# Last tiles one by one, earlier second gate and up weights, and a later weight turn in a four-stage network on one core

## The reference, cut to what matters

```python
x = x + ln(attn0(ln(x)))   # stage 1: per-token attention, Wq and Wkv
x = x + ln(ffn0(ln(x)))    # stage 2: ternary weights w1, w2, w3 (1408 hidden)
x = x + ln(attn1(ln(x)))   # stage 3: causal attention, 16 heads, RoPE
x = x + ln(ffn1(ln(x)))    # stage 4: gate and up 512x2048, 2:4 sparsified, down 2048x512

def quantize(w):           # of stage 2
    gamma = mean(abs(w))
    return clip(round(w / (gamma + 1e-8)), -1, 1)

def ffn1(x):
    h = silu(x @ w_gate) * (x @ w_up)
    h = keep_two_largest_of_every_four(h)      # by magnitude
    return h @ w_down
```

## Time and profile before

| | us |
|---|---|
| median of three runs | 1434.9 |
| range of the runs | 1433.83 to 1436.38 |
| the profiled execution | 1431.71 |
| its span, first to last instruction | 1430.0 |

### The profile page before, as it was taken

The page is one execution under the profiler, slowest core; times in us unless marked ns, Lnnn a source line. Parts: engine busy times, 40 slices in busy tenths (PEclk is TensorE's granted clock), DMA queues, the critical chain, the costliest instruction groups (busy, mean ns, idle before and its releaser), DMA issues.

```text
span 1430.0 us, 19458 instructions
## 1 busy us (share of the span) xinstructions
PE 1348.8 (94%) x7206; PEld 918.9 (64%) x7206; DVE 973.9 (68%) x1959; ACT 661.3 (46%) x1151; POOL 698.8 (49%) x836
## 2 busy tenths in 40 slices
PE   6988999999989899989999999999999999999996
PEld 5875445555455454555554447788888888888885
DVE  5997475755657776676665534577668767886776
ACT  6654233231314554445463574455454645454442
POOL 2676131421313323234243366487678768766863
PEclk9999999999999899999999999999999999999998
DMA  9100110203213111134020411522223232432300
GB/s 336 63 1 1 74 59 16 89 1 96 74 44 97 53 46 49 35 86 143 3 75 10 135 58 60 205 89 89 89 89 147 99 114 98 158 122 88 118 30 29
DMA packets 46270, 116.86 MB, mean 82 GB/s; under 512 B 3420, under 2 KB 4448, under 8 KB 42336
## 3 DMA queue, kind: packets, MB, share of 16 engines
q1 hardware_dynamic: 45104, 114.31, 23.8%
q10 hardware_dynamic: 1072, 1.31, 0.3%
HBM read 92.28 MB, written 23.07 MB: 81 GB/s over the span
## 4 chain that ended last, share of the span: by engine, by line
PE 65%; DVE 22%; ACT 5%; POOL 3%; issue 3%; DMA 1%; SPq 0%; POOLq 0%; DVEq 0%; ACTq 0%
PE PS L1657 63%; DVE cm L626 4%; DVE SM L642 3%; DVE PS L829 2%; DVE SM L638 2%; PE PS L1666 1%; DVE tm L626 1%; ACT EX L1241 1%; DVE hm L635 1%; DVE SM L643 1%; DMA rw<-in_L_ffn_w_up 1%; POOL xA L1472 1%; POOL SM L1472 1%; DVE SM L632 1%; DVE hm L626 1%
## 5 line engine op out<-in xcount | busy, mean ns | idle before, releaser
L1241 ACT ACTIVATE EX<-PS 128x512 f32<-128x512 f32 (+3 forms) x384 | 170.2, 495 | 154.9 <-PE PS L1657 153.9
L1472 POOL TENSOR_TENSOR ws_g<-rw,ws_g 128x512 fp32r<-128x512 f32 x64 | 138.5, 2164 | 124.8 <-ACT ws_g L1062 124.8
L1472 POOL TENSOR_TENSOR SM<-SM 128x1 f32<-128x1 f32 x128 | 82.5, 644 | 233.3 <-DVE SM L632 230.5
L1657 PE MATMUL PS<-KG,QG 96*128 96x512 f32 (+3 forms) x384 | 141.1, 392 | 21.5 <-DVE SM L829 9.0
L1576 POOL TENSOR_SCALAR_AFFINE_SELECT EX<-EX 128x128 f32<-128x128 f32 x256 | 75.3, 303 | 161.7 <-ACT EX L1241 158.3
L829 DVE CUSTOM_DVE_ANT_0 PS<-PS,MW 128x128 f32<-128x128 f32 (+3 forms) x256 | 122.4, 500 | 43.9 <-PE PS L1657 43.3
L1657 PE MATMUL PS<-QG,KG 98*128 98x512 f32 (+3 forms) x384 | 135.6, 382 | 3.2 <-ACT EX L1241 3.0
L1441 ACT ACTIVATE ab<-hm 128x512 f32<-128x512 f32 x64 | 40.5, 633 | 203.6 <-DVE hm L626 203.6
L1657 PE MATMUL PS<-ws_d,HH 128*128 128x512 f32 x528 | 125.7, 389 | 0.7 <-DVE HH L626 0.7
L638 DVE TENSOR_REDUCE SM<-PS 128x1 f32<-128x512 f32 x128 | 87.7, 686 | 55.4 <-PE PS L1657 55.1
L1657 PEld LDWEIGHTS PS<-QG,KG 98*128 98x128 f32 x384 | 72.0, 192 | 76.2 <-issue 45.3
(11 more groups left out here) (204 smaller groups left out, 2798.7 us busy)
## 6 DMA issues: line engine op xcount, KB each, us to landing
rw<-in_L_ffn_w_gate SPq DMA_DIRECT2D x16, 1024.0 KB, 5.1
rw<-in_L_ffn_w_up SPq DMA_DIRECT2D x16, 1024.0 KB, 5.1
rw<-in_L_ffn_w_down SPq DMA_DIRECT2D x16, 1024.0 KB, 6.9
QG<-qs SPq DMA_DIRECT2D x48, 256.0 KB, 4.5
raw<-in_L_ffn_w SPq DMA_DIRECT2D x3, 2816.0 KB, 11.7
qs<-stg SPq DMA_DIRECT2D x16, 512.0 KB, 3.5
xA<-xs SPq DMA_DIRECT2D x2, 2048.0 KB, 8.8
ys<-xA SPq DMA_DIRECT2D x4, 1024.0 KB, 5.9
```

The source lines that it names most:

```text
L1241: e.activation(EX[:, n % 16, 0:W], PS[:, score_bank(n), 0:W], ACT.Exp, scale=ISQ, bias=0.0).then_inc(S["ex"], 1)
L1472: return e.tensor_tensor(out, a, b, op)
L1657: return e.matmul(out, l, r, start=start, stop=stop, skip_group_check=free)
```

## The change

Four things change, and no instruction that computes is added or removed.

- **Turns at stage 2.** Blocks 0 and 1 of piece 11 of w3 are no longer turned at step 19. PE turns block 0 between `turn_x(1)` and `turn_x(2)` and blocks 1 and 2 after `turn_x(3)`. ACT copies all three after its four `turn_x`.
- **High and low parts first.** In each step of `project`, ACT's `out_hi` stands ahead of `norm6`, and DVE's `out_lo` ahead of the statistics.
- **Second gates and ups sooner; turns.** SP asks for g1 and u1 right after u0, ahead of the two row writes and the read of `xb[1]`. Their wait is now for the last weighing (`pvd` 96) and the last use of `RD` (`oo` 16). The first two turns of stage 4 (`turn4(0)`, `turn4(1)`) wait for the last exponential and no longer for the draining of the last weighed banks.
- **End.** PE runs the last four groups tile by tile. DVE takes the statistics of tile i+1 ahead of the addition of tile i, and those of tile 0 ahead of `last_low(1)`.

```diff
@@ sp_program
             w.wait_ge(S["st"], NS)
             e.dma_start(rw4[:, 1, :].rearrange("p (c i) -> p c i", c=4), wu_v[0]).then_inc(S["d_r1"], 16)
-            for half in range(2):
-                w.wait_ge(S["ey"], 8 + 4 * half + 4)
-                e.dma_start(ys_h[:, 8 + 4 * half:8 + 4 * half + 4, :],
-                            xc[:, 4 * half:4 * half + 4, :]).then_inc(S["d_ys1"], 16)
-
-            w.wait_ge(S["ot"], 16)
-            e.dma_start(xb[1][:, :, :], ys_h[:, 4:8, :]).then_inc(S["d_xb1"], 16)
...
                 else:
-                    w.wait_ge(S["ep"], 16)
+
+                    w.wait_ge(S["pvd"], 96)
+                    w.wait_ge(S["oo"], 16)
...
             ask("g", 1)
+            ask("u", 1)
+            for half in range(2):
+                w.wait_ge(S["ey"], 8 + 4 * half + 4)
+                e.dma_start(ys_h[:, 8 + 4 * half:8 + 4 * half + 4, :],
+                            xc[:, 4 * half:4 * half + 4, :]).then_inc(S["d_ys1"], 16)
+
+            w.wait_ge(S["ot"], 16)
+            e.dma_start(xb[1][:, :, :], ys_h[:, 4:8, :]).then_inc(S["d_xb1"], 16)
...
-                if s % 4 == 1:
+                if s % 4 == 1 and s > 1:
                     ask("u", s // 4 + 1)
@@ dve_program
             def project(step):
+                if 0 < step < 8:
+                    out_lo(1, step)
                 for k, i in stages(8, 4, step):
                     if k == 2:
                         w.wait_ge(S["ep"], 8 + i + 1)
                         stats(88 + i, PS[:, i % 4, :], EPS, "mv6")
-                    if k == 0 and i > 0:
-                        out_lo(1, i)
...
-            last_low(1)
-            for i in range(4):
+
+            def last_stats(i):
                 w.wait_ge(S["dd"], dd_at(63, i) - 3)
                 stats(124 + i, PS[:, i, :], EPS, "mv8")
+
+            def last_rows(i):
                 w.wait_ge(S["sn5"], 13 + i)
                 tt(xb[1][:, i, :], xb[1][:, i, :], row4("p", 12 + i), ALU.add).then_inc(S["xo"], 1)
+
+            last_stats(0)
+            last_low(1)
+            last_stats(1)
+            last_rows(0)
+            last_stats(2)
+            last_rows(1)
+            last_stats(3)
+            last_rows(2)
+            last_rows(3)
@@ act_program
-                if step < 21:
+                if step < 19:
                     quantized(step - 8, 0)
...
             def project(step):
+                if 0 < step < 8:
+                    out_hi(1, step)
                 for k, i in stages(8, 4, step):
                     if k == 3:
                         norm6(1, i, PS[:, i % 4, :])
-                    if k == 0 and i > 0:
-                        out_hi(1, i)
...
-            turn_x(0)
-            turn_x(1)
-            quantized(11, 1)
-            turn_x(2)
-            turn_x(3)
+            for i in range(4):
+                turn_x(i)
+            for part in range(2):
+                quantized(11, part)
@@ pe_program
-                quantized(s - 8, 0)
-                quantized(s - 8, 1)
+                if s < 19:
+                    quantized(s - 8, 0)
+                    quantized(s - 8, 1)
...
             def turn4(t):
                 w.wait_ge(S["sn4"], t + 1)
-                w.wait_ge(S["oe"], 16)
-                w.wait_ge(S["de"], 16)
+
+                w.wait_ge(S["ex"], NS)
+                if t >= 2:
+                    w.wait_ge(S["oe"], 16)
+                    w.wait_ge(S["de"], 16)
...
             turn_x(0)
             turn_x(1)
-            quantized(11, 2)
+            quantized(11, 0)
             turn_x(2)
             turn_x(3)
+            quantized(11, 1)
+            quantized(11, 2)
...
-            for half in range(2):
+            for i in range(4):
                 for q in range(60, 64):
-                    down4(q, (2 * half, 2 * half + 1))
+                    down4(q, (i,))
```

## The result

| | before | after |
|---|---|---|
| median of four runs, us | 1435.64 | 1421.63 |
| range of the runs | 1433.83 to 1437.64 | 1420.51 to 1426.00 |
| the profiled execution | 1431.71 | 1421.57 |
| its span | 1430.0 | 1419.8 |

The ratio after to before is 0.9899, with a 95% interval of 0.9876 to 0.9922: 14.0 us by the medians, 10.1 us by the two profiled executions. The forecast was 1422.2 us with a sum of 12.7 us. Timed again later beside the kernel before, the changed kernel was 9.7 us faster (1423.38 against 1433.12, ratio 0.9924), so the 14.0 us lie on the high side.

The account below looks back on a forecast made before the run. PE was taken to set the time from 931 us on, with losses at the entries of stages 4 and 2 and the tail. Gains 6.6 + 4.7 + 1.4 = 12.7 us gave 1434.9 - 12.7 = 1422.2 us, range 1418.0 to 1428.0.

Parts of the forecast that it names:

- Entry: Entry of stage 4: early asks and earlier PE start bring first comparison and ninth gate forward, gain 6.6 us.
- PE, not ACT, ends last, by 0.6 us: Stage 4 entry, ahead of the first comparison: PE's fourth up ends at 901.5, ACT's fourth silu at 900.9.
- The 3.1 us that ACT's order might have cost: Rival at stage 4 entry: high parts delay normalizations by 3.1 us, entry yields 3.5; 1425.3 us, chance 0.16.
- hidden: Rival at stage 4 entry: another equally long wait stands behind the transfers, entry yields 0; 1428.8 us, chance 0.07.
- PE alone: Rival: the comparison-to-ninth-gate chain shortens too and PE alone decides, 8.5 us at the entry; 1420.3 us, chance 0.08.
- End: After PE's last matmul: tile by tile, the last addition ends 3.6 us behind it; gain 4.7 us, 4 to 5.
- The step on the cover: End: tile 0's statistics, 1.09 us, fill DVE's idle time; without that cover PE's tile 2 is up to 1.1 late.
- Stage 2: Entry of stage 2: moved turns keep the clock up through the first 16 matmuls; gain 1.4 us, ends 1.6 and -0.5.
- the rests that are left there are under 1 us each: Ahead of stage 2's first dense matmul, two blocks of turns fill the 2.27 us idle time, leaving rests under 1 us.
- the clock takes back: Rival: clock falls at stage 2, gaining nothing, and at the last projection tile, losing 1.5 us; 1425.1 us, chance 0.20.
- The sum: Whole kernel: 6.6 + 4.7 + 1.4 = 12.7 us; profiled execution 1419.0, median of runs 3.2 above, 1422.2 us.
- Slower: Rival: granted clock stays at 0.50 over a long stretch of stage 4; 40 us of it give 1442, chance 0.02.

Follow-up runs that it names:

- an experiment: Changed kernel with ACT's split of the ninth gate weight ahead of group 5's absolute value and the third up weight's split a step later: 1421.79 us, ratio 0.9926.
- the eight later profiles of the other kind: Profiles with the changed kernel's end where PE's rest was 0.67 to 0.71 us and last 48 matmuls to last addition took 16.08 to 16.12 us.
- the unchanged kernel: The changed kernel run and profiled once more with no edit: 1423.38 us, ratio 0.9924 to the kernel before.
- the fill: Changed kernel with 14 unused matmuls of 512 columns added in PE's idle times around the third tile's turn at stage 2's entry: 1420.32 us, ratio 0.9918.
- the old splits: Kernels without the moved splits of the ninth gate weight and third up weight; the changed kernel with those moved took 1421.79 us, with the fill too 1421.60.

## Why the prediction was right or wrong

**Entry, right.** Forecast 6.6, measured 6.87. The step "PE, not ACT, ends last, by 0.6 us" is in the trace: DVE waits 4.61 us for PE's fourth up, and ACT's silu is over at 901.23, 1.4 us ahead of it. The first gate is 2.78 us sooner instead of 2.4, and the distance from comparison to ninth gate stayed (77.08 - 55.19 = 21.89; now 21.87), which is why the wait ahead of that gate became 1.54 us (forecast 1.9). The 3.1 us that ACT's order might have cost did not appear. The asks came later than forecast, 859.34 - 855.71 = 3.6 us behind the last weighing, since they wait for POOL's scaling; the transfers had landed by 867.04 and the first split of these weights starts at 894.67, so this cost nothing. The transfers were not hidden: the asks alone decide over 5.90 us.

**PE alone, wrong as a hope.** That rival wanted the chain behind the comparison to get shorter. It stayed at 21.9 us. When it was shortened in an experiment, 0.86 of the 1.21 us won at the gate were lost again behind it, where PE waits for DVE's products.

**End, right in its mechanism, lucky in its figure.** 4.7 forecast, 4.69 measured, 4.3 in the eight later profiles of the other kind. The forecast let the last round take 3.6 us behind PE's last matmul, as before; it took 1417.34 - 1413.30 = 4.0. In after that was made up by PE's rest, 0.32 us where the forecast kept 0.69, and that shorter rest belongs to the execution. The step on the cover, statistics of tile 0 in DVE's idle time, held, and its loss was seen where PE's order was taken back.

**Stage 2, wrong in the profile of after.** The forecast took 1.4 us and the first 16 matmuls became 0.63 us slower. The step that failed is "the rests that are left there are under 1 us each": those are 0.65 and 0.21 us, as forecast, but it counted only the rest ahead of `up2(0)` and the two blocks put into it, and set the 2.5 us that the cleared step 19 leaves ahead of the third turn apart as a condition of a rival. That rest is there, 2.21 us, and in seven of nine profiles the clock fell behind it. The rival *the clock takes back* was half right: at stage 2 it fell, at the last projection tile, after 1.20 us, it did not (12 matmuls in 2.97). Over ten profiles the part is worth 5.15 - 4.22 = 0.9 us on the mean (both profiles of the old order took 5.15), between -0.6 and 1.6, and no median shows it: it is a matter of the execution. The start of `up2(0)` was between 120.06 and 121.54 us in the twelve profiles with the turns moved and 120.40 and 120.24 in the two without, so the 0.63 lost there is within the spread.

**The sum.** 12.7 forecast less 2.66 for stage 2 (1.4 hoped for, 0.63 and 0.63 lost), plus 0.27 at the entry, less 0.16 in the stretches nothing touches, is 10.1. That the time came out at 1421.63 all the same is luck, because the second error has the other sign: the forecast added 3.2 us between the profiled execution and the median, and the profile of after took 1421.57, at its median. The profiled execution of before was a quick one of its kind, 3.9 us under the median of that comparison.

**Slower, did not come.** The clock was at 1.00 behind the ninth gate.

## What to carry over

A gain ahead of a wait is worth nothing until that wait is gone, so edits that lie on one path are costed together and tested by taking back one at a time: here 0.97 and 4.15 alone made 6.87 together, and of the end's two reorderings one alone gave nothing, the other about half. When work is moved out of one rest into another, the rest that it leaves is part of the bill: list every idle time of the engine after the move, the earlier ones too. For parts of one or two us, compare distances between points of the program, which repeated to 0.1 us at the entry here, and not the medians, whose runs spread over 2 to 7 us.

## What the runs showed of the hardware that was not expected

**The same rest, three outcomes of the clock.** After a rest of PE of 2.20 or 2.21 us, in the same order of work, the granted clock fell to 0.50 at one of two moments or not at all, and the first 16 matmuls took 3.5, 4.0 or 5.8 us. In both profiles that had the rest filled the clock stayed up. The Trainium skill, "TensorE: Matmul & The Clock Gate", section "What's actually happening", says of a kernel's start that the number of slow matmuls of one and the same kernel changes from run to run. In the middle of this one, the unchanged kernel's two profiles (5.78 and 3.51 us) agree, though in the second the rest was 1.37 us.

**The untouched stretch varies by more than any part of the change but the entry.** From `up2(1)` to the last weighing, where none of these kernels differ, the profiles took 727.8 to 733.5 us. The four longest, 733.2 to 733.5, are the four whose granted clock from 400 to 480 us is 0.87; the others have 0.91 to 0.96. The unchanged kernel profiled again, then the fill, both from 400 to 480 us:

```profile
400.00:480.00 80.00, 73.61 (x331) 42.20 (x332) 52.01 (x147) 28.44 (x53) 17.61 (x32) 0.87 0.27 73
```

```profile
400.00:480.00 80.00, 72.42 (x345) 39.81 (x350) 54.54 (x156) 29.39 (x55) 19.51 (x35) 0.96 0.27 73
```

That is why the smallest spans of all, 1416.8 and 1417.0 with the fill, don't show that it is a faster kernel.

**One meeting of DVE and POOL has two lengths, 3 us apart.** With the old wait of the turns, the stretch from the ninth gate to the last 48 matmuls took 478.79 us, against 475.5 to 475.8 in the others with the old splits. The loss lies at one change of chunks, where DVE's three comparisons took 9.85 us beside POOL's splits (in after, at the same place, 6.73), and PE then rested:

```profile
1090.88 9.85 DVE L630 TENSOR_TENSOR cm<-ab 128x1536 bf16<-128x1536 f32 x3 [0.70 <-ACT ab L1456]
```

```profile
1109.37 1.36 PE L1681 MATMUL PS<-idf,sl 128*128 128x128 f32 x8 [0.87 <-ACT sl L1081]
...
1115.39 2.97 PE L1672 MATMUL PS<-xT4b,ws_u 128*128 128x512 f32 x12 [1.76 <-DVE hm L630]
```

The edit is 230 us earlier. The same two lengths, 9.83 and 6.73 to 6.77 us, are those of the comparison at 1359.69 shown above, where PE did not wait for it in after; the unchanged kernel had both, so there no edit is needed. Whether the edit had a part in the meeting at 1090.88, one profile can't say.
